# A gated feed-forward layer with a per-sample style product, on one core: a rewrite of its quantising steps and of the order on every engine

## The reference

```python
w = weights[conditions]                       # 200 styles, 32 x 32 each
xc = einsum('bct,bcd->bdt', x, w)

def _act_quant(x):
    scale = 127.0 / clip(max(abs(x), axis=-1), 0.0001, None)
    return clip(round(x * scale), -128, 127) / scale
def _ternary_quant(w):
    s = mean(abs(w))
    return round(tanh(w / (s + EPS))) * arctanh(s)
def _linear_bit(x, w, g):                     # rmsnorm: g * x * rsqrt(mean(x*x) + EPS)
    return einsum('bsd,od->bso', _act_quant(_rmsnorm(x, g)), _ternary_quant(w))

h = silu(_linear_bit(xc, w1, g1)) * _linear_bit(xc, w2, g2)     # 1024 hidden
out = x + _linear_bit(h, w3, g3)
```

## Time and profile before

| | |
|---|---|
| median of 3 runs | 78.13 us |
| the three runs | 76.69, 78.13, 78.17 us |
| span of the profiled execution | 76.6 us; the page gives no time beyond it, it lies 0.1 under the fastest run |
| mean granted TensorE clock | 0.889 |
| busy: PE, VectorE (DVE), ScalarE (ACT), GpSimd (POOL) | 48.0, 58.1, 47.7, 55.4 us |
| share of the span | 63%, 76%, 62%, 72% |
| moved by transfers | 6.22 MB, nearly all before 24 us |
| first silu ends, last `hidden` ends | 35.6, 62.7 us |

### The profile page before, as it was taken

One profiled execution on the slowest core, in us unless ns is written; L12 is line 12 of the kernel. 1 busy time (PEld: TensorE's weight loads), 2 busy tenths in 40 slices (PEclk: granted clock), 3 DMA queues, 4 the chain that ended last, 5 costly groups with the idle time before them and its releaser, 6 DMA issues.

```text
span 76.6 us, 1068 instructions
## 1 busy us (share of the span) xinstructions
PE 48.0 (63%) x298; PEld 31.3 (41%) x302; DVE 58.1 (76%) x117; ACT 47.7 (62%) x70; POOL 55.4 (72%) x97
## 2 busy tenths in 40 slices
PE   0200509995829803999897298977888471079960
PEld 0200408774526702355461155544545250078730
DVE  0203278989999999967699989979797979996340
ACT  5014508599909995995859959896979783410000
POOL 6788777264938977989689898999999999810100
PEclk9999999999975895556999999999999999855589
DMA  0599989963710000000000000010202020010222
GB/s 0 119 385 346 327 237 278 330 210 115 253 71 0 0 0 4 0 9 4 0 0 0 0 0 4 17 52 9 68 0 68 0 68 0 23 45 0 68 68 68
DMA packets 5369, 6.22 MB, mean 81 GB/s; under 512 B 500, under 2 KB 4980, under 8 KB 5364
## 3 DMA queue, kind: packets, MB, share of 16 engines
q1 hardware_dynamic: 5108, 6.03, 24.6%
q0 software_dynamic: 256, 0.13, 0.8%
HBM read 5.11 MB, written 1.05 MB: 80 GB/s over the span
## 4 chain that ended last, share of the span: by engine, by line
DVE 24%; issue 22%; POOL 22%; DMA 12%; PE 11%; ACT 4%; SPq 0%; POOLq 0%; DVEq 0%
DMA w_sb<-in_L_ffn_w 12%; POOL hg L325 11%; PE y_ps L769 6%; DVE xg L477 6%; DVE cw_diag L446 5%; DVE x_peak L482 5%; PE a_ps L652 3%; PE t_ps L758 2%; POOL h_deq L302 2%; DVE hid L551 2%; ACT hr L413 2%; DVE abs_sum L438 2%; POOL h_root L316 2%; POOL h_base L311 2%; POOL h_base L309 1%
## 5 line engine op out<-in xcount | busy, mean ns | idle before, releaser
L325 POOL TENSOR_TENSOR hg<-hid,g_all 128x1024 f32<-128x1024 f32 x7 | 16.5, 2358 | 0.8 <-DVE hid L551 0.8
L413 ACT ACTIVATE hr<-hg,rounder,h_scale 128x1024 f32<-128x1024 f32 x7 | 8.7, 1241 | 5.5 <-DVE h_scale L574 5.5
L769 PE MATMUL y_ps<-w_t,hq_t 128*128 128x256 bf16 x64 | 10.3, 319 | 2.1 <-DVE hq_t L581 2.0
L560 DVE TENSOR_REDUCE h_peak<-hg 128x1 f32<-128x1024 f32 x8 | 9.7, 1217 | 1.7 <-POOL hg L325 1.6
L551 DVE SCALAR_TENSOR_TENSOR hid<-v_ps,x_deq,gate 128x1024 f32<-128x1024 f32 x8 | 10.2, 1271 | 0.9 <-PE v_ps L725 0.6
L725 PE MATMUL v_ps<-w_t,xq_t 128*128 128x512 bf16 x30 | 8.9, 415 | 3.0 <-DVE hid L551 2.9
L399 ACT ACTIVATE gate<-a_ps,x_deq 128x1024 f32<-128x1024 f32 x8 | 8.8, 1100 | 2.2 <-PE a_ps L725 2.1
L725 PE MATMUL a_ps<-w_t,xq_t 128*128 128x512 bf16 x30 | 8.7, 407 | 1.8 <-issue 1.3
L218 POOL DMA_INDIRECT cw_rows<-in_L_cond_weights,row_idx x8 | 7.9, 982 | 2.4 <-issue 2.1
L769 PEld LDWEIGHTS y_ps<-w_t,hq_t 128*128 128x128 bf16 x64 | 6.9, 115 | 5.6 <-DVE hq_t L581 4.1
L652 PE MATMUL a_ps<-x_sb,cw_diag 128*128 128x256 f32 x16 | 7.0, 597 | 2.5 <-DVE cw_diag L446 2.5
(11 more groups left out here) (76 smaller groups left out, 99.9 us busy)
## 6 DMA issues: line engine op xcount, KB each, us to landing
w_sb<-in_L_ffn_w SPq DMA_DIRECT2D x6, 512.0 KB, 4.5
x_sb<-in_x SPq DMA_DIRECT2D x4, 256.0 KB, 3.1
out<-x_sb SPq DMA_DIRECT2D x8, 128.0 KB, 1.7
g_all<-in_L_ffn_g SPq DMA_DIRECT2D x1, 512.0 KB, 4.3
g<-in_L_ffn_g SPq DMA_DIRECT2D x2, 128.0 KB
cw_rows<-in_L_cond_weights,row_idx POOLq DMA_INDIRECT x8, 4.3
cond_i<-in_itok_B SPq DMA_DIRECT2D x1, 0.1 KB
```

The costliest lines, as they stand in the source:

```text
L325: pool.tensor_tensor(hg[:, b], hid[:, b], g3_all[:], ALU.mult).then_inc(hg_ready, 1)
L413: act.activation(hr[:, t % 2], hg[:, t % 2], ACT.Identity, scale=h_scale[:, t % 2:t % 2 + 1], bias=rounder[:]).then_inc(hr_ready, 1)
L560: dve.tensor_reduce(h_peak[:, b], hg[:, t % 2], AX.X, ALU.max, apply_absolute_value=True).then_inc(hpeak_ready, 1)
L769: last = pe.matmul(y_ps[t % 2][:, 0:FEAT], hq_t[:, t % 2, j, :], w_t[2][:, j, :], start=(j == 0), stop=(j == KH - 1))
```

## The change

Nearly every line changes; the tiling and the three layers stay.

- **Styles.** Tiles 0 and 1 are gathered as before; then one indirect transfer gathers all 32 style matrices, 4 KB a row, SyncE stores them to a buffer in DRAM and reads them back by four strided transfers straight into the diagonal blocks of tiles 2 to 7. For tiles 0 and 1 one VectorE product with a mask replaces the copies.
- **Weights.** No tanh: `w / (2 atanh(1/2) (mean + EPS))` is written as int16 by one multiplication, which rounds it (`w_quantise`), and the value is cut to -1, 0, 1 after the transpose, by the sign on ScalarE or min and max on VectorE (`keep_w`). The weights are issued from ScalarE's queue, all six halves in a row, behind a table load.
- **Activations** are rounded by writing int16; EPS enters as one extra column in the sums of squares; the inverse root is one power of -1/2; scale is `min(127 / peak, inverse root)`.
- **Even and odd tiles.** GpSimd rounds and ScalarE keeps the even tiles, ScalarE rounds and VectorE keeps the odd ones; roots, scales and dequantisers are made for two tiles at once; the last tile is cut in halves between VectorE and ScalarE or GpSimd.
- **Order.** Only pair 0 of `x` is prepared before the first up product; pairs 1 to 3 are prepared within the main stretch, from an SBUF copy of the conditioned `x`, with the second gain on GpSimd. The new kernel's orders on GpSimd, ScalarE, VectorE and TensorE:

```diff
@@ sync
+            sp.wait_ge(all_in, 16)
+            sp.dma_start(cw_dram, cw_all[:]).then_inc(bounced, 16)
+            load_x(1)
+            sp.wait_ge(bounced, 16)
+            sp.wait_ge(diag_zero, 1)
+            for j in range(PER_TILE):
+                s = slice(j * CHAN, (j + 1) * CHAN)
+                sp.dma_start(cw_diag[s, EARLY:TILES, s],
+                             cw_dram.rearrange("(t j) (c d) -> j c t d", j=PER_TILE, c=CHAN)[j, :, EARLY:TILES, :]
+                             ).then_inc(cw_in, 16)
...
@@ gpsimd
+            def x_gain(p):
+                pool.wait_ge(xc_copied, p)
+                pool.tensor_tensor(xg[:, p, 1], xc[:, 2 * p:2 * p + 2, 0:FEAT],
+                                   g12[:, 1, :].unsqueeze(1).to_broadcast([P, 2, FEAT]), ALU.mult).then_inc(xg_p, 1)
+            def x_quant(p):
+                pool.wait_ge(xscale_ready, p + 1)
+                for i in range(2):
+                    pool.tensor_scalar(xq[:, p, 1, i], xg[:, p, 1, i], x_scale[:, p, 1, i:i + 1], 1.0,
+                                       ALU.mult, ALU.mult).then_inc(xq_done[p], 1)
+            def w_quantise(m, h):
+                pool.wait_ge(inv_ready, m + 1)
+                pool.tensor_scalar(half_of(m, h, w_q), half_of(m, h, w_sb), w_inv[:, m:m + 1], 1.0,
+                                   ALU.mult, ALU.mult).then_inc(w_quant[m][h], 1)
+            def quant(t):
+                pool.wait_ge(hscale_ready, t + 1)
+                if t >= 2:
+                    pool.wait_ge(h_turned[0], evens(t - 1))
+                pool.tensor_scalar(hq[:, 0], hg[:, t % 4], h_scale[:, t:t + 1], 1.0, ALU.mult, ALU.mult).then_inc(hq_done_p, 1)
...
+            w_quantise(0, 1)
+            x_inverse_rms(0)
+            w_quantise(1, 0)
+            w_quantise(1, 1)
+            x_gain(1)
+            w_quantise(2, 0)
+            x_inverse_rms(1)
...
+            gain(0)
+            x_quant(1)
+            x_dequant(1)
+            x_gain(2)
+            gain(1)
+            x_inverse_rms(2)
+            inverse_rms(0, 2)
+            x_gain(3)
+            gain(2)
+            x_quant(2)
+            x_dequant(2)
+            quant(0)
+            gain(3)
+            x_inverse_rms(3)
+            inverse_rms(2, 4)
+            pool.wait_ge(atanh_q_ready, 1)
+            dequant(0, 2)
+            gain(4)
+            x_quant(3)
+            x_dequant(3)
+            quant(2)
+            gain(5)
+            inverse_rms(4, 6)
+            dequant(2, 4)
+            gain(6)
+            quant(4)
...
@@ scalar
+            nc.scalar.preload_act_table_set("natural_log")
+            for m in range(3):
+                for h in range(2):
+                    act.dma_start(half_of(m, h, w_sb), half_of(m, h, w_rows)).then_inc(w_in[m][h], 16)
...
+            silu(0)
+            x_copy(1)
+            x_squares(1)
+            silu(1)
+            x_copy(2)
+            squares(0)
+            x_squares(2)
+            x_quant(1, 0)
+            x_copy(3)
+            silu(2)
+            squares(1)
+            x_squares(3)
+            x_quant(2, 0)
+            silu(3)
+            squares(2)
+            keep_h(0)
+            silu(4)
+            quant(1)
+            squares(3)
+            x_quant(3, 0)
+            for t in range(4, TILES, 2):
+                silu(t + 1)
+                squares(t)
+                if t + 2 < TILES:
+                    silu(t + 2)
+                keep_h(t - 2)
+                quant(t - 1)
+                squares(t + 1)
+            keep_h(6)
...
@@ vector
+            def x_scales(p):
+                dve.wait_ge(xpeak_ready, p + 1)
+                dve.reciprocal(x_inv[:, p], x_peak[:, p]).then_inc(xinv_ready, 1)
+                dve.wait_ge(xrms_ready, p + 1)
+                dve.wait_ge(xinv_ready, p + 1)
+                dve.scalar_tensor_tensor(x_scale[:, p], x_inv[:, p], QMAX,
+                                         x_rms[:, p].unsqueeze(1).to_broadcast([P, 2, 2]), ALU.mult, ALU.min
+                                         ).then_inc(xscale_ready, 1)
...
+            def scales(lo, hi):
+                dve.wait_ge(hpeak_ready, hi)
+                dve.reciprocal(h_inv[:, lo:hi], h_peak[:, lo:hi]).then_inc(hinv_ready, hi - lo)
+                dve.wait_ge(hinv_ready, hi)
+                dve.wait_ge(hrms_ready, hi)
+                dve.scalar_tensor_tensor(h_scale[:, lo:hi], h_inv[:, lo:hi], QMAX, h_rms[:, lo:hi], ALU.mult, ALU.min
+                                         ).then_inc(hscale_ready, hi - lo)
...
+            hidden(0)
+            x_gain(1)
+            x_peak_of(1)
+            hidden(1)
+            x_scales(1)
+            keep_w(2, 0)
+            keep_w(2, 1)
+            peak_of(0)
+            x_gain(2)
+            x_keep(1)
+            x_peak_of(2)
+            hidden(2)
+            peak_of(1)
+            x_scales(2)
+            scales(0, 2)
+            x_gain(3)
+            x_peak_of(3)
+            hidden(3)
+            x_keep(2)
+            peak_of(2)
+            x_scales(3)
+            keep_h(1)
+
+            hidden(4)
+            residual(0)
             x_keep(3)
+            peak_of(3)
+            scales(2, 4)
+            residual(1)
+            hidden(5)
+            peak_of(4)
+            keep_h(3)
+
+            hidden(6)
+            residual(2)
+            peak_of(5)
+            scales(4, 6)
+            residual(3)
+            hidden(7)
...
@@ tensor
+            up_a(0)
+            condition(1)
+            up_v(0)
+            up_a(1)
+            condition(2)
+            up_v(1)
+            w_turn(2, 0)
+            w_turn(2, 1)
+            condition(3)
             x_turn(1)
...
+            up_a(2)
+            up_v(2)
             x_turn(2)
+            up_a(3)
+            up_v(3)
+            h_turn(0)
+            up_a(4)
+            h_turn(1)
+            down(0)
+            up_v(4)
+            up_a(5)
             x_turn(3)
+            down(1)
+            up_v(5)
+            up_a(6)
+            h_turn(2)
+            h_turn(3)
+            down(2)
+            up_v(6)
+            up_a(7)
+            down(3)
+            up_v(7)
+            h_turn(4)
+            h_turn(5)
+            down(4)
+            down(5)
+            h_turn(6)
...
```

More of the change, by code:

```diff
@@ L630, in _ @@
-            peak_of(last)
-            step_of(last)
-            scale_of(last)
-            rounding_last(last)
-            keep_h(last - 1)
-            residual(last - 2)
-            keep_h(last)
-            residual(last - 1)
-            residual(last)
+            abs_sum_half(0, 1)
+            mean(0)
+            w_quantise(0, 0)
+            diagonal()
+            x_gain0(0)
+            x_gain0(1)
+            x_peak_of(0)
+            mean(1)
+            x_scales(0)
+            x_quant0()
@@ new lines, in _ @@
+            keep_w(0, 0)
+            abs_sum_half(2, 1)
+            x_keep(0)
+            mean(2)
+            arctanh()
+            x_dequant0()
+            keep_w(1, 1)
+            w_quantise(2, 1)
+            hidden(0)
+            x_gain(1)
[10 more added lines that the diff above has]
+            peak_of(1)
```

877 lines of the change are left out of this document (416 added, 461 removed).

## The result

The changed kernel takes 100.06 us in the median (99.61 to 101.01, four executions) where the kernel before, on the same chip, takes 77.47 (76.69 to 78.17): a ratio of 1.302, 95% interval 1.290 to 1.313. It is slower, as forecast, and by 10.6 us more than forecast; 100.06 lies above the range of 79 to 98. The profiled execution took 100.36 us, its span is 98.6 us and its mean granted clock 0.792.

The account below looks back on a forecast made before the run. GpSimd bounds the old main loop; waits in the new orders decide. Start 24.0 plus main stretch 59.5, clock 3.5 and collisions 1.7 give a span of 88.7; plus 0.8, 89.5 us. Own range 82 to 95 (0.63), wider range 79 to 98.

Parts of the forecast that it names:

- S: End of the first silu: forecast 24.0 us, bounds 22.2 to 27; before the change 35.6.
- The order: Main stretch: waits in the engines' new instruction orders decide; legs from the first silu to the end sum to 59.5 us.
- Three waits: On TensorE: x_turn(2) before up_a(3), h_turn(1) with down(0) before up_v(4), x_turn(3) before up_v(5); idle 6.6 us at x_turn(2), 3.6 at x_turn(3).
- Rival B: Main stretch: the order does not bind, GpSimd's own 40.6 us of work sets the end; 70 to 71 us, chance 0.11.
- The clock: TensorE slow after idling before x_turn(2), 2.2 us, and x_turn(3), 1.3: 3.5 us in all, ends 0 and 12.
- two collisions: In the start: 0.7 us added for two VectorE and GpSimd steps waiting each other out, raising 23.3 to 24.0.
- Collisions: Main stretch: VectorE steps with two SBUF inputs and GpSimd steps wait each other out; 1.7 us, ends 0 and 4.1.
- Hidden work: Style path: rows landed by 13, at most 19 us, wanted by condition(1) at about 20, so no cost.
- rival D: Style rows arrive late because 128-byte-run loads take twice 4.3 us, landing at 23; 92 to 93 us, chance 0.05.
- The int16 output: Rounding by int16 write, without a profile row: 1.13 us per 1024 elements on GpSimd; bounds 0 and +0.5 twice.
- Rival A: Main stretch: the clock stays low and every two-input step collides; 95 to 100 us, chance 0.16.

Follow-up runs that it names:

- experiments 1 to 3: Changed kernel, TensorE reordered: x_turn(2) behind up_v(3), 96.52 us; h_turn and down behind up_v(4) and up_v(6), 93.78; both plus x_turn(3) behind up_v(5), 89.08.
- experiment 4: Changed kernel with idle products on TensorE, results unused, in its idle times to hold the clock up: 91.69 us, ratio 1.182.
- Experiment 8: Changed kernel with weights issued from SyncE, later ones each behind a wait, x pair 0 behind the first layer's second half: 98.74 us median (96.35 to 99.75).
- experiment 7: Changed kernel with x pair 0 and the two gains issued in ScalarE's queue behind the first weight matrix: 99.65 us, ratio 1.272.
- experiment 6: Changed kernel with each element of x_scale, x_deq0 and h_scale as its own one-column instruction: 98.82 us, ratio 1.256.

## Why the prediction was right in direction and wrong in size

The legs of the prediction beside those of the changed kernel and of the run with the clock held up (from the start times of `hidden`; us):

| leg | forecast | measured | clock up |
|---|---|---|---|
| S, end of the first silu | 24.0 | 28.0 | 28.5 |
| S to hidden(3) | 20.2 | 24.9 | 22.1 |
| hidden(3) to hidden(4) | 7.7 | 9.1 | 7.8 |
| hidden(4) to hidden(5) | 7.7 | 8.2 | 8.0 |
| hidden(5) to hidden(6) | 6.35 | 8.6 | 6.2 |
| hidden(6) to hidden(7) | 3.45 | 4.05 | 4.1 |
| hidden(7) to the end | 14.1 | 15.8 | 13.4 |
| sum of the legs behind S | 59.5 | 70.6 | 61.5 |
| clock and collisions, as separate terms | 3.5 + 1.7 | within | collisions within |

The profiled 100.36 is 10.9 above 89.5, and it divides: S +4.0; the clock 70.6 - 61.5 = 9.0 in place of 3.5, +5.5; the legs at full clock 61.5 against 59.5 + 1.7, +0.3; the time around the span 1.8 in place of 0.8, +1.0. That last term was too small for both kernels: in every execution of which time and span are known, the kernel before's too, they lie 1.7 to 2.3 us apart.

**The order: right.** Three waits were read from the program, each placed and priced. Their lengths came out at 6.27 and 3.92 for 6.6 and 3.6; the leg sums at full clock are 61.5 against 61.2 with the collisions; and experiments 1 to 3 take out the first wait, the second, and all three together, for 3.5, 6.3 and 11.0 us. That the sums agree to 0.3 is in part luck: the leg to `hidden(3)` is 1.9 above its forecast, and the tail 0.7 below. Rival B, that the order does not bind, had the same engines' loads, which did fall; it is wrong. (Its GpSimd work, 40.6 us from 24.0, ends at 64.6 and not at 65.3, which changes nothing.)

**The clock: this term failed.** Its price was 3.5, with 12 as the upper end, and behind the start it measured 8.4 us in time and 9.0 in legs (experiment 4). The slow x_turn(2), up_a(3), up_v(3) were priced at 2.2, and that leg lost 2.8. But the idle time before x_turn(3) cost 0.2 there (8.2 against 8.0; its transposes took 0.62 after 3.92 us idle, and the slow up_v(5) behind them, 1.91 at 68.20, ended before VectorE was ready for it), while three legs for which I charged nothing lost 1.3, 2.4 and 2.4. The error was to charge the clock only behind the two waits of over 3 us. The row that I used against more, a wait of 1.58 us followed by a fast product, stood in a loop in which TensorE was busy for 68% of the time (40 to 46 us); here it is busy for 42% from 42.2 to 52.9 us and for 52 to 66% in the three legs behind, with waits of 2.2 to 2.7 us before h_turn, and the down products behind h_turn(1), (3) and (5) take 1.8 to 1.9 us each (the first at 59.05). The length of one wait doesn't decide it: the transposes of h_turn(4) took 0.62 after 2.51 us idle, those of h_turn(5) 1.03 after 2.15. What does is not separated by any run here. A slow product costs time where the order puts TensorE between ScalarE and VectorE, as in the legs that lost 1.3 and 2.4.

**The start: the second failed term,** 28.0 for 24.0 (bounds 22.2 to 27). The first product was put at 10.95 on the premise that x and the gains, fetched beside the weights, would be there. It began at 13.78, +2.8, because six halves of the weights in one queue made the load of x pair 0 take 8.6 us and the gathers 5.9. I had bounded how long the queue would be held back by a table load (0.9: it was not, the first half was issued at 0.82) and not what the queue does to the others. Experiment 8 gives 1.5 us of the 2.8 back; experiment 7 shows that it isn't x alone. The rest of experiment 8's 1.3 can be read from its trace: the diagonal starts 0.4 late, behind the gathers (5.3 us), takes 0.96 in place of 0.45 beside GpSimd's rounding, and x pair 0, issued at 7.26 and 4.9 us under way, lands 0.3 us behind it. The other 1.2 us of the start came behind the product, where 0.7 had been added for two collisions. These are x_scales(0), 1.04 us, and the first rounding, 1.45, where experiment 6 has 0.58 and 0.60; from the product to S it is 0.8 us shorter. The remaining 1.1 us is the clock again: x_turn(0) took 1.03 us for 0.6 and the second layer's transposes 1.91 for 1.2, and the forecast has no slow clock in the start outside its upper bound.

**Collisions: inside their bounds, the size not settled, the kind partly right.** Taken 1.7 of 4.1; the legs at full clock lie 2.0 above those without collisions, and experiment 6 takes out 1.2 to 3.6. x_scales(1) and (2) took 1.52 and 1.97 us in place of 0.16 (the one at 57.34, beside which GpSimd does nothing), gain(1) 2.80 in place of 2.35, x_quant(2) 1.43 in place of 0.95. A column of four elements waits out GpSimd's product as a whole tensor does. (The copy of 1.671 us that the prediction counts as a case of two SBUF inputs has one.) By the Trainium skill (SBUF — State Buffer, "Who interferes with whom") a VectorE instruction with two SBUF inputs contends with a GpSimd one that reads SBUF, and the reduce never does; both agree here, the eight `h_peak` have a mean of 1.21. But the term by its rule, 4.1, would have been 2.1 above those 2.0. Not foreseen was GpSimd's own wait of 2.08 at 42.73 for squares(1), which is behind silu(2) on ScalarE; in its place two pieces came out shorter (x_gain 1.09 for 1.25).

**Hidden work: right.** The style rows landed at about 18.0 (stored at 12.88, 1.9, four loads issued from 14.82, the last at 16.2, 1.7 each) and condition(1) first needs them at 25.2; rival D is wrong, short runs of 128 bytes cost no more than the 1.7 of a plain store. The int16 output had no row and cost nothing: 1024 elements took 1.11 us on GpSimd, 1.13 forecast. Rival A, the clock low and every step colliding at 95 to 100, is nearest to the outcome; half of it was true.

**Left open:** what lets TensorE's clock fall in one place and not in another, what the collisions cost in all, and whether an order exists in which the new scheme's seven tiles come near the 25.8 us of the kernel before. The best I wrote needs 38.4.
